# A sandwich of attention and channel mixing: the rest of the loops written out engine by engine

## The reference

```python
x = x + layernorm(attention(layernorm(x)))
x = x + layernorm(ffn(layernorm(x)))
# attention: q, k, v = split(x @ weight_qkv); softmax(q k^T / sqrt(256)) @ v; @ out_w.T + out_b
# ffn: xr, xk = mixes of x and the row before, with weights mu_r, mu_k
#      r = sigmoid(xr @ W_r.T); out = r * (square(relu(xk @ W_k.T)) @ W_v.T)
```

## Time and profile before

| | us |
|---|---|
| median of 3 runs | 855.45 |
| lowest and highest | 854.24, 855.83 |
| profiled execution, its own time | 853.94 |
| its span, first to last instruction | 851.8 |
| PE busy in it | 794.6 (93%) |
| DVE, POOL, ACT busy | 712.5, 550.8, 508.5 |
| mean granted clock of PE | 0.967 of 2.4 GHz |

### The profile page before, as it was taken

How to read it: one execution, slowest core, us unless ns; L and a number is a source line. 1 busy time by engine, 2 the same in 40 slices (tenths; PEclk the granted TensorE clock), 3 DMA queues, 4 the chain that set the end, 5 groups by cost and what they waited for, 6 DMA issues and landing times.

```text
span 851.8 us, 16118 instructions
## 1 busy us (share of the span) xinstructions
PE 794.6 (93%) x5749; PEld 572.5 (67%) x5749; DVE 712.5 (84%) x1805; ACT 508.5 (60%) x639; POOL 550.8 (65%) x717
## 2 busy tenths in 40 slices
PE   4879999999999999999999999999999999998664
PEld 3536767677776777677776776777777777777542
DVE  5698989988899998988889998988888888874553
ACT  3475556566566557766656557666666656655341
POOL 2110245677668777777768767777777777788761
PEclk9999999999999999999999999999999999999865
DMA  7565777477756864686648756775456646585100
GB/s 179 112 148 107 161 174 147 101 145 150 150 88 166 172 143 110 134 155 147 133 93 169 166 137 130 137 155 131 106 111 136 119 109 108 137 157 139 41 25 26
DMA packets 369312, 109.72 MB, mean 129 GB/s; under 512 B 342992, under 2 KB 368976, under 8 KB 369232
## 3 DMA queue, kind: packets, MB, share of 16 engines
q1 hardware_dynamic: 369232, 108.69, 61.0%
HBM read 18.75 MB, written 8.39 MB: 32 GB/s over the span
## 4 chain that ended last, share of the span: by engine, by line
PE 52%; DVE 30%; issue 8%; POOL 5%; ACT 2%; DMA 1%; SPq 1%; DVEq 0%; POOLq 0%; ACTq 0%
DVE probs L849 7%; PE M L1058 4%; PE M L1060 4%; PE M L1059 4%; PE S L1090 4%; PE S L1091 4%; PE S L1092 4%; PE S L1093 4%; PE S L1094 4%; PE Y L1111 4%; PE Y L1112 4%; PE Y L1113 4%; PE Y L1114 4%; PE Y L1115 4%; DVE p_lo L865 3%
## 5 line engine op out<-in xcount | busy, mean ns | idle before, releaser
L849 DVE TENSOR_SCALAR_CACHE_REDUCE probs<-S 128x512 f32<-128x512 f32 x256 | 173.2, 677 | 29.7 <-PE S L1094 29.5
L647 ACT ACTIVATE probs<-probs,exp_bias,kappa 128x2048 f32<-128x2048 f32 x64 | 133.6, 2088 | 51.3 <-DVE exp_bias L860 50.8
L865 DVE TENSOR_TENSOR p_lo<-probs,p_hi 128x2048 f16<-128x2048 f32 x64 | 151.5, 2367 | 3.1 <-ACT p_hi L597 3.1
L1112 PE MATMUL Y<-pt_lo,planes 128*128 128x256 f16 x512 | 140.2, 274 | 0.0
L1111 PE MATMUL Y<-pt_hi,planes 128*128 128x256 f16 x512 | 140.2, 274 | 0.0
L1113 PE MATMUL Y<-pt_hi,planes 128*128 128x256 f16 x512 | 140.2, 274 | 0.0
L1114 PE MATMUL Y<-pt_lo,planes 128*128 128x256 f16 x512 | 140.1, 274 | 0.0
L1115 PE MATMUL Y<-pt_hi,planes 128*128 128x256 f16 x512 | 140.0, 273 | 0.0
L597 ACT ACTIVATE p_hi<-probs 128x2048 f16<-128x2048 f32 x64 | 121.5, 1899 | 21.8 <-DMA pt_lo<-p_lo 21.8
L1090 PE MATMUL S<-turned,q_hi 128*128 128x512 f16 x256 | 97.9, 382 | 8.2 <-DVE q_lo L840 5.1
L541 POOL TENSOR_TENSOR xm_lo<-mixed,xm_hi 128x512 f16<-128x512 f32 x62 | 99.9, 1611 | 4.2 <-ACT xm_hi L597 4.1
(11 more groups left out here) (184 smaller groups left out, 2005.9 us busy)
## 6 DMA issues: line engine op xcount, KB each, us to landing
x_res<-in_L_attn_x SPq DMA_DIRECT2D x32, 256.0 KB, 3.0
out_x<-gate SPq DMA_DIRECT2D x32, 256.0 KB, 2.3
xs<-in_L_attn_x SPq DMA_DIRECT2D x28, 128.0 KB, 2.9
xs<-in_L_attn_x SPq DMA_DIRECT2D x14, 256.0 KB, 3.3
pt_hi<-p_hi SPq DMA_TRANSPOSE x64, 4.0
pt_lo<-p_lo SPq DMA_TRANSPOSE x64, 4.0
mxt<-mx SPq DMA_TRANSPOSE x31, 3.3
pt_hi<-in_L_attn_weight_qkv SPq DMA_DIRECT2D x3, 128.0 KB, 2.6
```

The costliest lines, as they stand in the source:

```text
L647: act.activation(probs[:, h % 2, t, :], probs[:, h % 2, t, :], ACT.Exp, bias=exp_bias[:, t:t + 1], scale=kappa[:, 0:1], accum_out=row_sum[ ...
L849: dve.tensor_scalar(probs[:, h % 2, t, c * BLK:(c + 1) * BLK], S[k % RING][:, :], 1.0, None, ALU.mult, ALU.max, accum_out=chunk_max[:, t, ...
L865: dve.tensor_tensor(p_lo[:, t, :], probs[:, h % 2, t, :], p_hi[:, t, :], ALU.subtract).then_inc(p_lo_made, 1)
L1112: pe.matmul(to[:, 0, :], low, p_l, start=False, stop=final, skip_group_check=True)
```

## The change

1. `SLOTS` becomes `UNITS * H` = 256: the loops end with the last scores. What is left of every engine is written out call by call (36 calls on PE, 69 on DVE, 40 on POOL, 40 on ACT and 17 on SP).
2. In what is written out, heads 27 to 31 are turned by PE and ACT (`turn_mix_in`, `mix_in_out`), not by DMA: `mix_high`, `mix_low`, `turn_mix` and `mix_in_sum` fall away for heads 27 to 30. Part of the work of these heads moves from POOL and ACT to DVE.
3. From head 26 (`KEYS_LEFT`) the keys use bank S[0], from head 25 (`FEED_LEFT`) the feed uses S[1]. These are free once all scores are copied. So the receptance waits for its reader `rec_made` and no longer for `gated`, and the projection for no keys.
4. The turned probabilities of head 31 go to tiles that batch 2 has left, not to the pair that head 29 uses.
5. In the loops `GATE`, `GATE_STATS` and `GATE_RSQRT` move one slot up (59, 60, 61), and on DVE `gated` stands ahead of `probs_low`. `GATE_NORM` stays.
6. The semaphores of `mixed`, `xm_hi` and `xm_lo` are split in one for receptance and one for keys; waits are added where the written order needs them.

```diff
-    GATE = 60
-    GATE_STATS = 61
-    GATE_RSQRT = 62
+    GATE = 59
+    GATE_STATS = 60
+    GATE_RSQRT = 61
...
-    SLOTS = UNITS * (H - 1) + STORE + 1
-
-    DRAIN = H - 1
+    SLOTS = UNITS * H
+    LEFT = H - 8
+    MIX_LEFT = H - 6
+    TURN_LEFT = H - 5
+    KEYS_LEFT = H - 6
+    FEED_LEFT = H - 7
...
+        KEYS_LEFT_BANK, FEED_LEFT_BANK = S[0], S[1]
...
             def receptance(h):
-                pe.wait_ge(xm_lo_made, h * 2 + 1)
-                if h >= 1:
+                pe.wait_ge(xm_lo_made[0], h + 1)
+                if h >= KEYS_LEFT:
+                    pe.wait_ge(rec_made, h)
+                elif h >= 1:
                     pe.wait_ge(gated_made, h)
...
             def split_high(h, i):
                 if h >= 1:
-                    act.wait_ge(key_done, h)
-                act.wait_ge(mixed_made, h * 4 + 2 * i + 2)
+                    act.wait_ge(rec_done if i == 0 else key_done, h)
+                act.wait_ge(mixed_made[i], (h + 1) * HALVES)
...
+                if (h := at(k, GATE)) is not None:
+                    gated(h)
                 if (ht := exp_at(k, FIRST_LOWER, LOWER)) is not None:
                     probs_low(*ht)
```

PE, behind its loop (H is 32, so H - 7 is head 25; `values(h, a, b)` is units a to b - 1):

```diff
+            turn_mix_in(H - 5)
+            project_out(H - 4, KEYS_LEFT)
+            values(H - 3, 1, 5)
+            mix_keys(H - 6, 0)
+            values(H - 3, 5, 8)
+            receptance(H - 6)
+            values(H - 2, 0, 2)
+            project_out(H - 3, KEYS_LEFT)
+            values(H - 2, 2, 4)
+            turn_mix_in(H - 4)
+            values(H - 2, 4, 5)
+            feed(H - 7)
+            values(H - 2, 5, 8)
+            feed(H - 6)
+            receptance(H - 5)
+            project_out(H - 2, KEYS_LEFT)
+            mix_keys(H - 5, 0)
+            values(H - 1, 0, 5)
+            turn_mix_in(H - 3)
+            feed(H - 5)
+            mix_keys(H - 4, 0)
+            values(H - 1, 5, 8)
+            turn_mix_in(H - 2)
+            receptance(H - 4)
+            project_out(H - 1, KEYS_LEFT)
+            mix_keys(H - 3, 0)
+            feed(H - 4)
+            receptance(H - 3)
+            mix_keys(H - 2, 0)
+            feed(H - 3)
+            receptance(H - 2)
+            turn_mix_in(H - 1)
+            feed(H - 2)
+            mix_keys(H - 1, 0)
+            receptance(H - 1)
+            feed(H - 1)
```

DVE, behind its loop, from the projection of the last head on:

```diff
+            attention(H - 1)
+            attention_stats(H - 1)
+            mix(H - 2, 0)
+            gated(H - 4)
+            attention_norm(H - 1)
+            add_attention(H - 1)
+            residual_stats(H - 1)
+            gated_stats(H - 4)
+            gated(H - 3)
+            mix_in(H - 1)
+            gate_norm(H - 4)
+            gated_stats(H - 3)
+            differences(H - 1)
+            mix(H - 1, 1)
+            mix(H - 1, 0)
+            split_low(H - 1, 1)
+            split_low(H - 1, 0)
+            gated(H - 2)
+            gated_stats(H - 2)
+            squares_low(H - 1)
+            gated(H - 1)
+            gated_stats(H - 1)
+            gate_norm(H - 1)
+            finish(H - 1)
```

More of the change, by code:

```diff
@@ L408, in _ @@
                     load_residual(h)
+            turn_high(H - 2, 1)
+            load_residual(H - 3)
+            store(H - 8)
+            turn_low(H - 2, 1)
+            turn_high(H - 1, 0)
+            load_residual(H - 2)
+            turn_high(H - 1, 1)
+            turn_low(H - 1, 0)
+            turn_low(H - 1, 1)
+            store(H - 7)
+            load_residual(H - 1)
+            store(H - 6)
+            store(H - 5)
+            store(H - 4)
+            store(H - 3)
+            store(H - 2)
+            store(H - 1)
             for i in range(2):
@@ L1053, in _ @@
                         weight_low(2 * i + 1)
+            inverse_sums(H - 2)
+            mix(H - 6, 0)
+            mix(H - 6, 1)
+            differences(H - 5)
+            attention(H - 4)
+            attention_stats(H - 4)
+            split_low(H - 6, 1)
+            mix(H - 5, 1)
+            inverse_sums(H - 1)
+            probs_low(H - 1, 0)
+            split_low(H - 6, 0)
+            mix(H - 5, 0)
+            residual_stats(H - 4)
+            attended_low(H - 3)
+            probs_low(H - 1, 1)
+            mix_in(H - 4)
+            attention(H - 3)
+            attention_stats(H - 3)
+            mix(H - 4, 1)
+            mix(H - 4, 0)
+            gated(H - 7)
+            squares_low(H - 6)
+            gated_stats(H - 7)
+            attended_low(H - 2)
+            gated(H - 6)
+            gate_norm(H - 7)
+            gated_stats(H - 6)
+            attention(H - 2)
+            attention_stats(H - 2)
+            split_low(H - 4, 0)
+            residual_stats(H - 3)
+            attention_norm(H - 2)
+            squares_low(H - 5)
+            mix_in(H - 3)
+            add_attention(H - 2)
+            residual_stats(H - 2)
+            gated(H - 5)
+            mix(H - 3, 1)
+            gated_stats(H - 5)
+            mix_in(H - 2)
+            mix(H - 3, 0)
+            gate_norm(H - 5)
+            attended_low(H - 1)
+            differences(H - 2)
+            mix(H - 2, 1)
+            attention(H - 1)
[22 more added lines that the diff above has]
+            finish(H - 1)
         @block.tensor
@@ L1117, in attend, with values @@
                     mm.then_inc(pv_done, 1)
+            def values(h, first, end):
+                for kt in range(STEPS * first, STEPS * end):
+                    attend(h, kt)
             def by_rows(to, a_hi, a_lo, w, done):
@@ L1197, in _ @@
             for k in range(SLOTS):
-                if k < H * UNITS:
-                    scores(k)
+                scores(k)
                 for v in range(UNITS):
                     if (h := at(k, VALUES + v)) is not None:
-                        for kt in range(STEPS * v, STEPS * (v + 1)):
-                            attend(h, kt)
+                        values(h, v, v + 1)
                 if (h := at(k, PROJECT)) is not None:
-                    project_out(h, k)
-                if (h := at(k, TURN)) is not None and h >= DRAIN:
-                    turn_mix_in(h)
+                    project_out(h, begun(k, KEYS))
                 if (h := at(k, RECEPT)) is not None:
```

297 lines of the change are left out of this document (211 added, 86 removed).

## The result

The changed kernel takes 832.69 us (median of 4, 831.39 to 833.72) beside 854.85 us for the kernel before (4 runs, 854.23 to 855.83): a ratio of 0.9756, with a 95% interval of 0.9739 to 0.9773, 22 us faster. Forecast were 828, with a range of 819 to 841; the measured time is 4.7 us above the forecast. The profiled execution took 831.39, with a span of 829.6.

The account below looks back on a forecast made before the run. PE bounds the loops, a latency chain the tail: 749.0 + 58.4 + 7.1 + 3.2 + 7.95 = 825.7, + 4 for collisions - 5.6 for loops = 824.1 span, 827.8 with execution offsets, so 828 us; range 819 to 841.

Parts of the forecast that it names:

- The bound and where to look: Loops bound by PE, only its pauses count (6.6 us); tail of 103.8 us a latency chain, waits 23.7, clock 15.2.
- signs named for being wrong: POOL or DVE over 85% mid-tail with PE awaiting `xm_lo` or `sq_lo`; store ahead of `gated`; last scores at 748 or later.
- Loops, a gain of 5.6 us: From 100 to 748 us, `gated` one slot earlier removes PE's nine pauses, 6.6 us, less 1 for pauses filled by other engines.
- the first rival: Loop pauses go elsewhere and their gain doesn't come, tail as forecast: 833.6 us, chance 0.14.
- Tail, work of PE 58.4: PE's remaining matmuls and transposes from 749.0 us, including 2.6 us more for transposing heads 27 to 30: 58.4 us.
- Tail, waits 7.1: PE's waits in the written-out tail: 1.5 + 0.6 + 1.8 + 3.2 = 7.1 us, in place of 23.7.
- an allowance of 4: Tail: 4 us for some 30 DVE steps slowed by POOL at 0.6 each, out of 0 to 18 us.
- The walk: Following all five engines' written order through the tail with profiled durations, which gave PE's waits station by station, 7.1 us.
- The half clock, 3.2: End of the tail: only the last 30 matmuls at half clock, costing 3.2 us in place of 15.2.
- After the last matmul 7.95: End of the tail: the same DVE and POOL steps and a store follow the last matmul, staying at 7.95 us.
- Spare banks at no gain of their own, added waits at nothing: Tail: no separate bank term in the sum; added waits cost nothing, except 1 to 2 us for `gated` if POOL's queue slips.
- Slower, by the score copy behind `gated`: Loops: the score copy behind `gated` and `probs_low` stops PE in each head; 868 us at 1.2 a head, chance 0.03.

Follow-up runs that it names:

- The gate's move alone: Kernel before with only GATE 59, GATE_STATS 60, GATE_RSQRT 61 and `gated` ahead of `probs_low`: 856.78 us, 1.0043 of the kernel before.
- Behind `probs_low` the same move: Changed kernel with all three gate constants kept one slot up, but `gated` behind `probs_low` on DVE: 827.70 us, 0.9697 of the kernel before.
- The two runs at the chain's end: Changed kernel, GATE 59 behind `probs_low`, GATE_STATS 61, GATE_RSQRT 62; last attention norm on ACT, with or without head 31's differences ahead of head 29's `gated_stats`: 829.12, 828.82 us.
- the gate's old place: Changed kernel with GATE 60, GATE_STATS 61, GATE_RSQRT 62 and `gated` behind `probs_low`, written-out tail untouched: 829.86 us, 0.9726 of the kernel before.
- only `gated` moved: Changed kernel with GATE 59 behind `probs_low`, GATE_STATS 61 and GATE_RSQRT 62 as in the kernel before: 827.47 us, 0.9687 of the kernel before.
- the end of the chain changed: Against the changed kernel with GATE 59 behind `probs_low`, GATE_STATS 61, GATE_RSQRT 62: last attention norm on ACT, head 31's differences before head 29's `gated_stats`: 829.12 us, 0.9716.

## Why the prediction was right, point by point

- **The bound and where to look: right.** The tail's waits and its clock were what could be won, and they gave all of the gain. One of the signs named for being wrong came all the same: the last scores at 748 or later (748.3, 742.4 forecast). Another came in part: DVE was busy for 89% of the first 46.7 us of the tail, and PE waited 0.9 us for `sq_lo` in them.
- **Loops, a gain of 5.6 us: wrong**, a loss of 1.3 to 1.9 in its two profiles. This is the step that failed. Of the nine pauses for `gated` two of 0.3 are left. The step said that `probs_low` and the copy are late by `gated`'s 0.68 and no more. It priced the move by the queue of DVE, and did not ask what starts on POOL in those 0.68 us; it even had `xm_lo` 0.7 later, where it is shorter now (1611 to 1258 ns) and `p_lo` pays. The row that tells it was there, `p_lo` at 258.66 and `xm_lo` at 259.00, an order that 0.34 us decide. `p_lo` grew by 0.37 us in the mean, in place of `xm_lo`, and DVE was at 94 to 97% in the stretches with new rows of x. Against the first rival I held that two thirds of the heads have no pause; it came out near its number (833.6, measured 832.7). The gate's move alone, 0.4% slower, shows it without the rest. Behind `probs_low` the same move gains 2.5 to 2.8 us in the loops, half of what was forecast. The Trainium skill (SBUF — State Buffer, Who interferes with whom) says "Issue order, not op shape, decides who blocks"; the two timelines agree, POOL's 3.20 us before and DVE's 3.12 after.
- **Tail, work of PE 58.4: right.** The four further sets of transposes took 0.6 to 0.7 each.
- **Tail, waits 7.1 and an allowance of 4: right in sum.** Measured 11.6. The walk had the places: 2.3 (1.5 expected) for the first `mix_in`, 0.9 (0.3) at the feed of head 26, 0.3 at the transpose of head 29, 0.6 (0.7) for the keys of head 30, 2.2 (0.6) for the transpose of head 31, 3.2 (2.7) for its keys, 1.3 (0.5) for the last feed, 0.4 (0.5) for the feed of head 30, and 0.4 at the last projection, where none was expected. The allowance was for meetings of DVE and POOL. The norm and the addition on the last chain, 3.8 us for 1.5, are such a piece; for the rest of what the walk had too short no run tells the cause. The two runs at the chain's end show that such a meeting moves to the next step as its neighbour is taken away.
- **The half clock, 3.2: 1.6 measured.** The keys of head 31 took 2.74 us and the receptance 1.83, where 1.48 is full speed; the last feed had the whole clock. Which steps fall in it differs: with the gate's old place the feed of head 30 had it (2.74) and the keys did not (1.48), which is 1.3 us of that kernel's shorter tail; whether that belongs to the kernel or to the one execution is not shown.
- **After the last matmul 7.95: 7.2.** The sum by the measured terms, from 749.2: 58.4 + 11.6 + 1.6 + 7.2 = 828.0, against 829.6; the waits are counted from the modelled end of a matmul, about 0.16 us behind the start of the next one in a row, nine times. In the sum for the kernel before these pieces were inside the term for the clock (busy time less 0.109 a matmul); the forecast of the tail left them out. So that the tail came out at 81.3 us, with 81.7 forecast, is in part luck: the clock and the end were 2.4 us better than forecast, the waits 0.5 and the part left out 1.4 worse.
- **Spare banks at no gain of their own, added waits at nothing: right** as far as measured; the stores delayed no `gated`.
- **Slower, by the score copy behind `gated`:** from 100 us on PE never waits for a score copy; what it waits for is `q_lo` and `y_lo`. The gate's move alone costs 3.4 us in the whole, not the 27 that this rival needed.

## What to carry to other kernels

Where two engines can hold each other up, the rows to read are not their busy shares but which of two steps starts first, and by how little; moving an instruction past the holder can turn that round, and the cost appears as a longer instruction, not as a wait. In this kernel a freed bank or a shorter way was worth little while the order of issue stayed (0.1% and 0.4%, 0.7% together), and most of the gain came with the written-out order and what it moves (2.0%). In a chain of short steps at the end, a step moved ahead can be paid for by the next queue that it makes late. Before two profiles are compared by the time of a late event, compare them at an event that the edit can't have reached: here they differed by 1.7 us there, as much as the loss that was looked for.

## What the runs showed that was not expected

- Moving `gated` by one statement, with all else equal, is worth 0.5 to 0.6% (0.9747 and 0.9756 against 0.9697), though DVE executes the same instructions.
- A small step of POOL can be held as long as a large one: in the kernel before, an addition of two numbers a partition took 2.26 us (764.22) beside `p_lo`, once, and 0.19 to 0.20 in 30 of its 32 times.
- A DVE norm with one tile as input, in and out in SBUF, was held too: 2.10 us, where `mix_in`, of the same form, takes 0.73 in the two halves together.
- Executions of one kernel differ by up to 5 us (823.7 to 828.8 with only `gated` moved). The profiles of two kernels with the same loops (only `gated` moved, and that with the end of the chain changed) differ in PE's clock between 25 and 60 us, 0.98 and 0.91, and in the time of the last scores, 744.1 and 745.9. Slot 24 begins at 66.7 and 68.4 in them, and from there on they take the same time (677.4 and 677.5).
